# A Gram product with one sample per matmul in four column tiles instead of two samples in two

## What is computed

```python
e = stack([tbl_f[ids[:, f]] for f in range(27)], axis=1)      # 2048 x 27 x 128
interactions = einsum('bfd,bgd->bfg', e, e)                   # the Gram of each sample
x = interactions.reshape(B, 27 * 27)[:, TRIL_IDX]             # f > g
h = concatenate([bottom, x, bottom], axis=1)                  # 2048 x 607
h = maximum(h @ W_top1 + b_top1, 0)                           # 512
h = maximum(h @ W_top2 + b_top2, 0)                           # 256
y = h @ W_top3                                                # 1
```

## Time and profile before

| | us |
|---|---|
| median of 3 runs | 400.92 |
| lowest, highest | 399.76, 405.23 |
| profiled execution, its own time | 399.54 |
| span of its instructions | 397.7 |
| PE busy in the span | 350.3 |
| DVE busy | 232.7 |
| ACT busy | 139.1 |
| POOL busy | 271.3 |
| mean granted clock of TensorE | 0.97 of 2.4 GHz |

### The profile page before, as it was taken

One profiled execution on the slowest core, in us unless ns is written; L12 is line 12 of the kernel. 1 busy time (PEld: TensorE's weight loads), 2 busy tenths in 40 slices (PEclk: granted clock), 3 DMA queues, 4 the chain that ended last, 5 costly groups with the idle time before them and its releaser, 6 DMA issues.

```text
span 397.7 us, 10200 instructions
## 1 busy us (share of the span) xinstructions
PE 350.3 (88%) x4224; PEld 329.4 (83%) x4224; DVE 232.7 (59%) x292; ACT 139.1 (35%) x267; POOL 271.3 (68%) x288
## 2 busy tenths in 40 slices
PE   0568687998999899998999899998999899998847
PEld 0558677998899889997899889998899889998745
DVE  2889948971788346941788346942698176832000
ACT  2333352143523332153523342155413351344312
POOL 6777777777777777777777777777777777710050
PEclk9998699999999999998999999999999999998969
DMA  8999564337342534345332634244332734302120
GB/s 179 213 235 223 162 212 142 106 72 226 69 111 67 194 93 109 70 122 164 79 103 61 190 97 111 68 126 154 80 99 61 221 69 113 68 21 47 35 28 2
DMA packets 46942, 45.76 MB, mean 115 GB/s; under 512 B 34862, under 2 KB 37481, under 8 KB 46001
## 3 DMA queue, kind: packets, MB, share of 16 engines
q1 hardware_dynamic: 35380, 26.09, 25.6%
q0 software_dynamic: 9024, 17.91, 17.3%
q10 hardware_dynamic: 2492, 1.12, 1.0%
HBM read 39.52 MB, written 5.55 MB: 113 GB/s over the span
## 4 chain that ended last, share of the span: by engine, by line
PE 80%; DMA 7%; DVE 4%; ACT 3%; issue 3%; SPq 1%; ACTq 1%
PE work L329 38%; PE gram L358 13%; PE work L401 7%; PE work L341 7%; PE work L386 5%; PE work L388 4%; PE work L387 4%; DVE onehot L469 3%; PE work L409 2%; DMA misc<-in_tbl 2%; DMA h<-in_tbl 2%; DMA inter<-in_tbl 2%; DMA grams<-inter 2%; DVE tab_lo L454 1%; DVE x_lo L494 1%
## 5 line engine op out<-in xcount | busy, mean ns | idle before, releaser
L301 POOL DMA_INDIRECT emb<-in_tbl,ids_all x272 | 264.9, 974 | 84.1 <-issue 80.2
L469 DVE TENSOR_TENSOR onehot<-ids_bc,row_idf 125x512 fp32r<-125x512 int32 (+1 forms) x224 | 195.8, 945 | 31.4 <-PE work L329 30.3
L329 PE MATMUL work<-onehot,tab_hi 125*128 125x256 f32 x672 | 170.6, 294 | 22.4 <-DVE onehot L469 21.2
L329 PE MATMUL work<-onehot,tab_lo 125*128 125x256 f32 x672 | 167.3, 288 | 0.0
L329 PEld LDWEIGHTS work<-onehot,tab_hi 125*128 125x128 f32 x672 | 132.4, 197 | 24.6 <-issue 17.7
L329 PEld LDWEIGHTS work<-onehot,tab_lo 125*128 125x128 f32 x672 | 132.5, 197 | 0.0
L543 ACT COPY embT<-work 128x512 f32<-128x512 f32 x40 | 29.9, 804 | 121.2 <-PE work L329 121.2
L358 PEld LDWEIGHTS gram<-embT 128*54 128x54 f32 x2048 | 53.5, 130 | 9.5 <-issue 7.5
L358 PE MATMUL gram<-embT 128*54 128x52 f32 x2048 | 56.6, 214 | 2.5 <-ACT embT L438 2.0
L386 PE MATMUL work<-x_hi,w_hi 128*128 128x256 f32 (+1 forms) x128 | 39.5, 309 | 16.3 <-DVE x_lo L494 16.3
L494 DVE TENSOR_TENSOR x_lo<-misc,x_hi 128x256 fp32r<-128x256 f32 (+1 forms) x24 | 8.9, 418 | 67.8 <-ACT x_hi L563 67.8
(11 more groups left out here) (33 smaller groups left out, 119.0 us busy)
## 6 DMA issues: line engine op xcount, KB each, us to landing
ids_bc<-in_sel_ids SPq DMA_DIRECT2D x7, 1280.0 KB
grams<-inter SPq DMA_DIRECT2D x64, 84.5 KB
emb<-in_tbl,ids_all POOLq DMA_INDIRECT x272
inter<-in_tbl SPq DMA_DIRECT2D x3, 448.0 KB
h<-in_tbl SPq DMA_DIRECT2D x3, 448.0 KB
ids_bc<-in_sel_ids SPq DMA_DIRECT2D x5, 256.0 KB, 9.1
misc<-in_bottom SPq DMA_DIRECT2D x8, 128.0 KB
misc<-in_tbl SPq DMA_DIRECT2D x2, 448.0 KB
```

The costliest lines, as they stand in the source:

```text
L301: pool.indirect_dma_start(out=emb[:, t % TILE_SLOTS, f, :], out_offset=None, in_=gather_tables[f], in_offset=bass.IndirectOffsetOnAxis(ap= ...
L329: mm = nc.tensor.matmul(out, part[0:k, CHUNK_AT[f] + c, :], onehot[0:k, at % RING, i * HALF:(i + 1) * HALF], start=(c == 0 and i % 2 == 0 ...
L469: nc.vector.tensor_tensor(onehot[0:k, at % RING, 0:width], ids_bc[0:k, four[0]:four[-1] + 1, :].rearrange("p i n -> p (i n)"), row_idf[0:k ...
```

## The change

A matmul of the Gram has one sample: 27 columns of weights, 26 moving ones, a result of 27 partitions by 26 columns. The four samples of a group go to partitions 0, 32, 64 and 96, so the array works as four column tiles of 32. Every product is of use. A group now takes 26 columns of `gram` instead of 52, so `SPAN` is 16, `GRAMS` 2, and a copy takes 123 partitions by 26 x 16. `inter` is [26, 32] for each partition, in a buffer that is as large as the longest staged table wants. The stores read partitions 32q+1 to 32q+26. All of `gram` is zeroed at the start, since partitions 27 to 31 of each quad are copied too.

```diff
-SPAN = 8
+SPAN = 16
...
     GRAMS = P // QUADS // SPAN
-    TWO = QUADS // 2
-    SIDE = P // 2
-    ROWS = SIDE + TWO * NF
-    COLS = TWO * NG
+    ROWS = (QUADS - 1) * QS + NF
...
-        inter = sb("inter", [P, COLS, QS])
+        inter_stage = sb("inter", [P, max(NG * QS, max(CHUNKS) * D)])
+        inter = inter_stage[:, 0:NG * QS].rearrange("p (g n) -> p g n", g=NG)
...
-        gram = ctx.enter_context(nc.psum_tensor("gram", [P, 2, SPAN, SIDE], F32))
+        gram = ctx.enter_context(nc.psum_tensor("gram", [P, 2, SPAN, QS], F32))
...
                 for q in range(QUADS):
-                    row, col = q // TWO * SIDE + q % TWO * NF, q % TWO * NG
-                    sp.dma_start(grams[t, q, 1:NF, :, :], inter[row + 1:row + NF, col:col + NG, :]).then_inc(stored, 16)
+                    sp.dma_start(grams[t, q, 1:NF, :, :], inter[q * QS + 1:q * QS + NF, :, :]).then_inc(stored, 16)
...
                     for q in range(SPAN):
                         a = (u * SPAN + q) * QUADS
-                        for side in range(2):
-                            two = embT[:, t % 2, a + side * TWO:a + (side + 1) * TWO, :]
-                            last = nc.tensor.matmul(gram[side * SIDE:side * SIDE + TWO * NF, n % 2, q, 0:COLS], two.rearrange("d s f -> d (s f)"),
-                                                    two[:, :, 0:NG], start=True, stop=True)
+                        for i in range(QUADS):
+                            one = embT[:, t % 2, a + i, :]
+                            last = nc.tensor.matmul(gram[i * QS:i * QS + NF, n % 2, q, 0:NG], one, one[:, 0:NG], start=True, stop=True)
                     last.then_inc(grammed, 1)
...
-                products(2 * h + 1, range(2))
+                products(2 * h + 1, range(GRAMS // 2))
...
-                products(2 * h + 1, range(2, GRAMS))
+                products(2 * h + 1, range(GRAMS // 2, GRAMS))
...
-            dve.memset(gram[P // QUADS:SIDE, :, :, :], 0.0).then_inc(gram_zeroed, 1)
+            dve.memset(gram[:, :, :, :], 0.0).then_inc(gram_zeroed, 1)
...
                 nc.scalar.copy(inter[0:ROWS, :, u * SPAN:(u + 1) * SPAN],
-                               gram[0:ROWS, n % 2, :, 0:COLS].rearrange("f q g -> f g q")).then_inc(extracted, 1)
+                               gram[0:ROWS, n % 2, :, 0:NG].rearrange("f q g -> f g q")).then_inc(extracted, 1)
```

More of the change, by code:

```diff
@@ L172, in dlrm_tower @@
         longest, short = max(CHUNKS) * D, min(CHUNKS) * D
-        stage = [inter[:, :, :].rearrange("p c n -> p (c n)"), h1[:, :, :].rearrange("p m n -> p (m n)"), misc]
-        assert longest <= COLS * QS and longest <= (CH + 2) * HALF and D * (HALF // P) == HALF
+        stage = [inter_stage, h1[:, :, :].rearrange("p m n -> p (m n)"), misc]
+        assert longest <= (CH + 2) * HALF and D * (HALF // P) == HALF
         assert short <= M1 * HALF and all(CHUNKS[i] * D <= short for n, i in enumerate(TABLE_ORDER) if n % STAGE == 1)
@@ L619, in _ @@
                     extract(2 * h + 1, u)
-                    if h and u == 1:
+                    if h and u == GRAMS // 2 - 1:
                         result(h - 1)
```

## The result

The kernel with the change takes 452.69 us (median of 4 runs, 449.45 to 455.27) against 400.34 (4 runs, 398.40 to 405.23) for the one before: ratio 1.130, 95% interval 1.123 to 1.136. It is slower by 52 us. The mean granted clock fell from 0.97 to 0.908.

What follows compares the result with a forecast made beforehand. TensorE, busy 88% of the span and carrying 80% of the chain, was taken to bound the kernel. Gram pace 5, late instruction blocks 26 and clock 8 sum to 39 us on a median of 400.9: 440 us, range 406 to 465.

Steps and rivals of the forecast that it cites:

- (1): Gram on TensorE: twice the matmuls at half the width cost 13.75 ns a record, +5 us over 16 tiles.
- rival D: Gram: four records under way at a time and instruction blocks hidden, -22 us, 379 us in all; chance 0.06.
- E: Gram: four records at a time, but with stalls for late instruction blocks, 430 us; chance 0.10.
- how many are under way at a time: Gram records overlapping on TensorE: taken as two; four, 7 ns a record, -22 us, was only the low end.
- rival B: Gram: a fixed 25 ns a record whatever its width, +51 us, few stalls, 452 to 462 us; chance 0.22.
- (2): Gram: twice the instructions, so blocks of 256 arrive late and TensorE stalls, +26 us (5 to 47).
- The time from trigger to use: Gram: from entering one instruction block to having the next, 4.6 us in even tiles, 3.1 in odd ones.
- The time that a block lasts: Gram: 256 instructions at 13.75 ns a record are eaten in 1.8 us.
- the tenth taken off for tiles where the grid is kind: Gram: stall sum of 29 us cut by a tenth for kindly placed block edges, giving +26 us.
- (3): TensorE's clock: stalls in and after even Grams bring about five more stretches at 0.50, +8 us (0 to 14).
- (4) to (7): ScalarE's 32 copies of 0.51 us, unchanged stores, the larger memset and `inter`'s size: 0 us in the sum.
- The premise on GpSimd: GpSimd's gathers of table rows: they leave 80 us between them; no term in the sum.

Runs made afterwards that it cites:

- onetile: Changed kernel with all four samples of a group written to partitions 0 to 26, one column tile, result of no use: 466.16 us against 399.24, ratio 1.171.
- idslate_b: Changed kernel with the 1280 KB load of selected ids put behind the even tile's stores from the second half on: 435.49 us against 399.24, ratio 1.089.
- half_b: Changed kernel with every second group of four samples left out of the Gram: 386.30 us against 399.24, ratio 0.968; on the slower chip 647.64 us, 0.967.
- after: The kernel with the change, one sample a matmul in four column tiles, against the kernel without it: 452.69 us, ratio 1.130.
- before: The kernel without the change, the base of every comparison: 400.34 us, or 668 to 670 us on the slower kind of chip.
- pad: Kernel without the change, plus a one-column by one-column matmul behind each matmul of the Gram: 1044.92 us against 670.19 on the slower chip, ratio 1.564.
- early: Kernel without the change, only ScalarE's rounding of the packed pairs moved ahead of the even tile's copies: 653.52 us against 668.12 on the slower chip, ratio 0.978.

## Why the prediction was right or wrong

The sign and the range held (452.7 within 406 to 465; slower had 0.80). The forecast of 440 was 12.7 us short. By its steps:

**(1) The pace of the Gram: size right by luck, reason wrong by a factor of two that other costs filled.** Predicted 13.75 ns a record, +5 us. The short spacings of the Gram sum to 54.6 us for 4096 records, 13.3 ns each, +0.7. But this is no cost by width. The array takes such a record every 6.9 ns when the instructions are there (28 spacings, the first of a Gram), which is rival D's and E's rate. In 15 of the 16 Grams this ends after 34 records; from there a load and a matmul come every 8.3 ns, about 4.2 ns an instruction, which I read as the supply. Behind a hole, at a clock of 0.50, the burst itself has 11.7 ns a record. And 59 small holes of 0.12 to 0.6 us sum to 14.1 us, 3.4 ns a record.

The small holes go with GpSimd's gathers. Between the loads of the Grams there are 66 of 0.12 to 0.45 us, and 57 of them end 0.1 to 0.2 or 0.6 to 0.7 us after a gather has started. The last two Grams, beside which no gather runs, take 2.2 and 2.6 us without their long hole, 8.5 and 10 ns a record, where the others take 3.0 to 4.2. No run takes the gathers away, so that they cause the small holes is argued from the times alone.

Cost by width was right inside one column tile: 54 columns take 50 ns there (25 in two tiles), 27 columns 27.5 (onetile). The step that failed is the value taken for "how many are under way at a time": it stayed at two, though the change makes them four, which the sum had only as its low end. D's argument, that the two tiles of before overlap, was right; E, four at a time with late blocks, came nearest to the mechanism, and I gave the two 0.16 together. Both missed that the array's gain of 26 us can't be had in full, since the instructions aren't there.

**(1, rival B) A fixed 25 ns a record: refuted as the mechanism, though its 452 to 462 holds the result.** With it there would be 25 ns and no holes; there are 13.3 ns and holes of 38 us. The rule of the Trainium skill that the prediction weighed ("TensorEngine Tiling (Array Packing)", Performance Considerations, Instruction Overhead, about 60 cycles a matmul) is near onetile's 27.5 ns a record, but the 6.9 ns of a burst in four tiles are below it: here it can at most hold for each column tile by itself.

**(2) The late blocks: right in kind and place, too small.** Predicted one hole in every Gram at a place that repeats every 256 instructions, longer in even tiles, 29 us less a tenth. In the trace all 16 holes lie at the same place modulo 256, if TensorE's semaphore instructions are counted with its loads and matmuls; in order of time they are 6.5, 3.95, 4.1, 4.2, 2.6, 3.4, 4.0 and 1.8 us in even tiles (30.6) and 0.45 to 1.7 in odd ones (8.0). The mean of an even hole is 3.8 where I had 2.8. An odd one is 1.0 where I had 0.8.

Three terms of the sum were off. The time from trigger to use: from the first instruction of the block in front of a hole to the first one behind the hole it is 2.9 to 8.2 us in even tiles, 5.5 on the mean, where I had 4.6 (5.7 in the tile shown above), and 2.9 to 3.8, 3.5 on the mean, in odd ones, where I had 3.1. From the packet's start to the first instruction it is 2.2 to 2.8 us at all 16, as read from two; what varies is when the packet starts, 0.6 to 1.4 us after its block is entered in odd tiles and 2.0 to 5.9 in even ones, the last apart. The time that a block lasts: I had 1.8 us, which holds in even tiles (1.7 on the mean), but in odd ones it is 2.5, since layer 3 stands inside that block in seven of eight. And the tenth taken off for tiles where the grid is kind: there is none, since a tile's 512 instructions hold two edges wherever the grid lies, and each of the 16 Grams has its hole. The Trainium skill's "mostly hidden" ("Runtime: NRT & Kernel Launch", Instruction fetch mechanics) is true of all other stages: one hole of 1.02 us in select, none in layers 1 to 3.

The cause of most of the even tiles' excess was not in the prediction at all: the 1280 KB of ids in front of the block's packet. Moving them took 11.2 us of holes away in the six tiles concerned. With them moved, it is 3.6 us from entering a block to having the next in the even tiles of the later halves, so the 4.6 that I took stands between the wait without that transfer in front and the wait with it.

**(3) The clock: right in kind, 5 us too small.** Predicted +8 (0 to 14). Layer 1's short spacings rose by 13.1 us: 192 of its records are at 0.50 and come 219 ns apart, the others 126, and before it was 53. The time at 0.50 went from 23.9 to 81.9 us in the whole; every even tile has 6.8 to 10.2 us of it, where I had five more stretches of 3.4. It falls with the time for which TensorE stands still in the Grams: 65.1 us in idslate_b, 10.2 in onetile_b, where the Gram is worked steadily. The holes aren't all of it: half_b has none in its Grams, half of the Gram's work, and still 44.4 us at 0.50 and 61.2 us in layer 1.

```profile
152.70:162.90 10.20, 6.55 (x121) 6.43 (x122) 1.09 (x3) 1.42 (x4) 7.45 (x8) 0.50 0.35 93
```

This is the stretch behind one hole: 10.2 us at 1.2 GHz, all of it through the Gram's rest, the wait for ScalarE and the start of layer 1.

**(4) to (7) Copies, stores, memset, inter: as predicted, nothing.** 32 copies of 505 ns (predicted 0.51); "everything else" sums to 1.7 us less in after than in before.

**The premise on GpSimd: wrong, without effect on the forecast.** "Its gathers leave 80 us between them" took the earlier trace rows as free time. It is 263 pauses of 0.3 us between back-to-back gathers, and after a pause GpSimd isn't free: in before it waits for TensorE for 2.4 us in all, and 272 x (0.97 + 0.30) = 345 us nearly fills the time up to its last gather, at 349.5. The transposes of the last tile start about 15 us after that, which is all the slack there is. So a kernel that gains more than some 15 us on TensorE meets GpSimd, as half_b did, and D's 379 would have been about 386 even with hidden blocks (an estimate, 401 less these 15). The waits of after show the other side: it waits for TensorE 40.5 us now, since TensorE is late.

```profile
POOL emb L298 <- issue: 78.9, 259, 0.3
...
POOL emb L298 <- PE work L338: 40.5, 12, 5.8
```

The sum that would have been right is 0.7 (pace) + 38 (blocks) + 13 (clock) = 52, less 2 elsewhere: 50, the difference of the spans. So the forecast held with a pace term that fitted by luck and two terms that were about a third too small, all from a mechanism, late blocks of 256, that the holes, onetile and the moved load bear out.

## What to carry to other kernels

Where many small matmuls replace few, count instructions before array time: an instruction block lasts only as long as its work, so put beside each stage the time that 256 instructions last there and compare it with the time from trigger to use, read at a place where the trace shows one late (here 3 to 6 us). Look also at what transfer is issued just ahead of that place. More column tiles raise the array's pace only as far as instructions are supplied (here 13 ns for a record with its load, 8.5 where nothing disturbed it); beyond it, fewer and wider matmuls were the better trade here. Before counting on a gain, see how much slack the next engine really has by its first and last work and by the releasers of its pauses, not by its idle share.

## What the runs showed of the hardware

- **Column tiles add up.** 27.5 ns a record in one, 14 to 15 in two, 6.9 in four (fp32, 27 columns of weights, 26 moving).
- **Wide and one-column matmuls in turn are slow.** 366 ns for each added one (pad, at a mean clock of 0.65 and on the slower kind of chip). No run shows why.
- **The supply of instructions.** About 4.2 ns an instruction, and at every 256 a wait that is 0.45 to 6.5 us long in a Gram. A block was usable 2.2 to 2.8 us after its packet had started (152.34 to 154.88 in the tile shown) and 2.9 to 8.2 us after the block before it was entered; a 1280 KB transfer issued just ahead made about 2 us of that.
- **Small holes beside gathers.** Two for each gather of GpSimd, of 0.2 to 0.3 us, at the same two places of its cycle of 1.25 us, and none in the last even Gram, where no gather runs.
- **Two kinds of chip.** On three of the chips the kernel before takes 668 to 670 us instead of 400, with the same program. Select mostly keeps its 15.55 us there (16.2 to 16.7 in half) and layer 2 its 27.3 in all; the mean granted clock is 0.79 for 0.97. The instructions of the Gram come late one by one. The loads of half in a part of such a Gram (start us, us, instruction, idle before):

```profile
94.53 0.12 PEld L355 LDWEIGHTS gram<-embT 128*27 128x27 f32 x1 [0.58 <-issue]
95.94 0.12 PEld L355 LDWEIGHTS gram<-embT 128*27 128x27 f32 x1 [1.29 <-issue]
96.65 0.12 PEld L355 LDWEIGHTS gram<-embT 128*27 128x27 f32 x1 [0.59 <-issue]
98.13 0.12 PEld L355 LDWEIGHTS gram<-embT 128*27 128x27 f32 x1 [1.36 <-issue]
```

  The loads' starts are 0.7 us or twice that apart. The waits of early, there, are `PE gram L358 <- issue` 193.1 us in 165 pieces, where the trace of before on a chip of 400 us has 7.5 us for the loads and none for the matmuls. This too goes with the gathers: all 162 spacings over 0.6 us between the loads of the Grams of early end while gathers run or at most 4.1 us after one, and the Gram of tile 14, beside which none runs, takes 3.4 us there as it does on a chip of 400 us. What links the two, on either kind of chip, stays open; a kernel without gathers would be the next run.
